# A graph convolution on one core: filters laid out by edge through TensorE alone, messages kept in SBUF, gathers released by the row sums

## What is computed

```python
def reference(x, src, dst, edge_attr_50, ...):
    h = jnp.maximum(_layernorm(x), 0.0)
    W = silu(edge_attr_50 @ fw1 + fb1) @ fw2 + fb2      # a filter for each edge, 50 -> 128 -> 128
    y = silu(h @ aw1 + ab1) @ aw2 + ab2                 # the node table
    msg = W * y[src]
    agg = jax.ops.segment_sum(msg, dst, num_segments=6250)
    out = silu(agg @ ow1 + ob1) @ ow2 + ob2
    return x + h + out
```

## Time and profile before

| what | value |
|---|---|
| time, median of 3 (lowest, highest) | 2037.55 us (2035.7, 2040.6) |
| span of the profiled execution, first to last instruction | 2356.9 us |
| POOL busy in it | 1526.1 us, 65% |
| PE busy in it | 1290.8 us, 55% |
| DVE busy in it | 1191.7 us, 51% |
| ACT busy in it | 520.7 us, 22% |
| TensorE clock granted, mean | 0.741 of full speed |

### The profile page before, as it was taken

The page is one execution under the profiler, slowest core; times in us unless marked ns, Lnnn a source line. Parts: engine busy times, 40 slices in busy tenths (PEclk is TensorE's granted clock), DMA queues, the critical chain, the costliest instruction groups (busy, mean ns, idle before and its releaser), DMA issues.

```text
span 2356.9 us, 13198 instructions
## 1 busy us (share of the span) xinstructions
PE 1290.8 (55%) x4526; PEld 700.7 (30%) x4526; DVE 1191.7 (51%) x1497; ACT 520.7 (22%) x545; POOL 1526.1 (65%) x1619
## 2 busy tenths in 40 slices
PE   3454555655565557555655565555564566554645
PEld 2222333332232323223322232222232233322323
DVE  4455445555455445544544564445444454444545
ACT  3322222222121122122212221222121122121211
POOL 5556666667666666666666666666666676666665
PEclk9686777777786768776877786777686777677867
DMA  4421222212221212212212221222221222212211
GB/s 148 144 76 45 82 58 71 79 51 85 82 83 45 83 50 81 87 46 81 86 51 78 80 85 50 80 65 65 82 85 48 82 54 81 85 45 82 59 46 44
DMA packets 62293, 171.47 MB, mean 73 GB/s; under 512 B 27088, under 2 KB 29648, under 8 KB 59024
## 3 DMA queue, kind: packets, MB, share of 16 engines
q0 software_dynamic: 51584, 105.75, 16.8%
q1 hardware_dynamic: 8192, 61.32, 6.9%
q10 hardware_dynamic: 2448, 3.54, 0.4%
HBM read 164.08 MB, written 6.42 MB: 72 GB/s over the span
## 4 chain that ended last, share of the span: by engine, by line
another core or an unknown queue 30%; POOL 24%; PE 18%; issue 16%; ACT 9%; DVE 2%; DMA 0%; SPq 0%; POOLq 0%; ACTq 0%; DVEq 0%
POOL xg L381 24%; PE banks L884 9%; PE banks L876 4%; ACT hid L444 4%; ACT hid L450 4%; PE banks L891 2%; PE banks L824 1%; PE banks L899 1%; ACT hs L469 0%; DVE stats L557 0%; PE banks L819 0%; DMA xs<-in_x 0%; PE banks L944 0%; DVE sums L668 0%
## 5 line engine op out<-in xcount | busy, mean ns | idle before, releaser
L381 POOL DMA_INDIRECT xg<-node_table,src x1564 | 1479.0, 946 | 777.6 <-issue 451.3
L884 PE MATMUL banks<-hid,wts 128*128 128x512 f32 x806 | 534.4, 798 | 556.3 <-ACT hid L444 437.9
L665 DVE TENSOR_TENSOR banks<-banks,xg 128x1024 f32<-128x1024 f32 (+1 forms) x198 | 241.4, 1219 | 1070.2 <-DMA xg<-node_table,src 607.2
L668 DVE TENSOR_REDUCE sums<-banks 128x128 f32<-128x1024 f32 (+1 forms) x408 | 494.0, 1211 | 13.7
L876 PE MATMUL banks<-attr,wts 50*128 50x512 f32 x806 | 284.4, 786 | 383.1 <-ACT hid L450 206.4
L444 ACT ACTIVATE hid<-banks,cols 128x1024 f32<-128x1024 f32 x202 | 224.7, 1112 | 887.9 <-remote 672.4
L450 ACT ACTIVATE hid<-banks,cols 128x1024 f32<-128x1024 f32 x202 | 224.6, 1112 | 865.6 <-remote 376.6
L884 PEld LDWEIGHTS banks<-hid,wts 128*128 128x128 f32 x806 | 180.6, 249 | 746.6 <-ACT hid L444 465.7
L891 PE MATMUL banks<-ident,hid 128*128 128x128 f32 x1612 | 283.5, 333 | 40.1 <-issue 38.1
L891 PEld LDWEIGHTS banks<-ident,hid 128*128 128x128 f32 x1612 | 224.6, 170 | 237.1 <-issue 228.6
L672 DVE TENSOR_TENSOR banks<-banks,other 128x1024 f32<-128x1024 f32 (+1 forms) x204 | 248.7, 1219 | 7.0
(11 more groups left out here) (83 smaller groups left out, 282.9 us busy)
## 6 DMA issues: line engine op xcount, KB each, us to landing
attr<-in_attr SPq DMA_DIRECT2D x25, 2048.0 KB
xg<-node_table,src POOLq DMA_INDIRECT x1564
out<-res ACTq DMA_DIRECT2D x8, 256.0 KB
xs<-in_x SPq DMA_DIRECT2D x3, 512.0 KB, 6.6
node_table<-res SPq DMA_DIRECT2D x3, 512.0 KB
out<-res ACTq DMA_DIRECT2D x5, 192.0 KB
spare<-in_dst SPq DMA_DIRECT2D x1, 808.0 KB
src<-in_src SPq DMA_DIRECT2D x1, 808.0 KB
```

What stands on the lines that cost most here:

```text
L381: pool.indirect_dma_start(xg[:, i % XG, j, :], None, table[:, :], bass.IndirectOffsetOnAxis(ap=src[:, s * L + j:s * L + j + 1], axis=0))\
L665: dve.tensor_tensor(to, to, rows_of, ALU.mult).then_inc(signal, 1)
L668: return dve.reduce_sum(sums[:, at, m, :], of.rearrange("p j f -> p f j"), AX.X)
L884: i = pe.matmul(hid_ps[:, at], w["fw2_s"][:, :], hid[:, s % 2, at], start=True, stop=True)
```

## The change

It does five things.

1. `filters` now makes the filters by edge directly. For each tile of 128 edges the hidden values are the stationary operand and `fw2` the moving one, 128 wide, eight matmuls into `fil_ps[s % 2]`. The bias comes first, as two bf16 matmuls 512 wide of a row block `fb2_rows` that holds `fb2` in three bf16 parts. `by_edge` (the transposes) and ScalarE's `add_fb2` go, and with them `across`, `biased` and `fil_done`.
2. The hidden layer runs `FILL` = 2 pairs ahead. One semaphore, `pe_turn`, is added to once a turn, by `hidden(s + 2)`, which stands behind `filters(s)`; all who waited for one of TensorE's semaphores in the loop wait for it, the node MLP's steps too (`turn_of`, `after`).
3. The message is written over the gathered rows in `xg` (in `e_x` for early pairs) in SBUF, and masked there; both row sums read it there.
4. `filters(s)` waits for `msg_done` of pair `s - 2`, and `pair_sums(a)` for `red_done` of its own pair. POOL waits for `red_done` of the pair that last used its buffer, three sets back, and no longer for the filters of the pair before.
5. `fb2_rows` is built on VectorE at the start, ahead of the node statistics (eight small instructions and a wait for the `rows` load); before, this stood in the fallback.

```diff
@@ POOL
                 if i >= XG:
-                    pool.wait_ge(fil_done, run(s - REACH))
+                    pool.wait_ge(red_done, run(MAIN_TURNS[i - XG]))
@@ ScalarE
-                for a in ((0, 1) if s == 0 else (s + 1,)):
+                for a in range(FILL + 1) if s == 0 else (s + FILL,):
                     if a < PAIRS:
                         silu_hid(a)
-                        add_fb2(a)
@@ VectorE, head
+            dve.wait_ge(s_rows, 16)
+            dve.wait_ge(s_set, 1)
+            dve.tensor_copy(fb2_part[:, 0, :], rows[:, 0, :]).then_inc(s_fb2, 1)
+            dve.wait_ge(s_fb2, 1)
+            dve.tensor_tensor(fb2_rest[:, 0, :], rows[:, 0, :], fb2_part[:, 0, :], ALU.subtract).then_inc(s_fb2, 1)
...
+            for i in range(3):
+                dve.tensor_copy(fb2_rows[32 * i:32 * i + 1, :, :],
+                                fb2_part[32 * i:32 * i + 1, i:i + 1, :].to_broadcast([1, TPG, F])).then_inc(s_fb2, 1)
@@ VectorE, loop
-            def message(to, rows_of, signal):
-                dve.tensor_tensor(to, to, rows_of, ALU.mult).then_inc(signal, 1)
+            def message(to, filters_of, signal):
+                dve.tensor_tensor(to, filters_of, to, ALU.mult).then_inc(signal, 1)
...
-                dve.wait_ge(fil_done, run(s))
-                msg = by_tile(s, 0, L)
-                message(msg, rows_of, msg_done)
+                dve.wait_ge(pe_turn, after(s))
+                msg = rows_of
+                message(msg, by_tile(s, 0, L), msg_done)
@@ TensorE
                 if s > 0:
-                    pe.wait_ge(biased, run(s - 1))
+                    pe.wait_ge(hid_done, run(s - 1))
...
-                i.then_inc(hid_sum, 1)
+                i.then_inc(pe_turn, 1)
             def filters(s):
+                to, halves = fil_ps[s % 2], range(tiles_in(s) // TPG)
+                pe.wait_ge(msg_done, run(s, LAG))
+                for h in halves:
+                    pe.matmul(to[:, GC * h:GC * h + GC], ones_b[:, :], fb2_rows.rearrange("p j f -> p (j f)"), start=True, stop=False)
                 pe.wait_ge(hid_done, run(s))
-                for h in range(tiles_in(s) // TPG):
-                    at = slice(GC * h, GC * h + GC)
-                    i = pe.matmul(hid_ps[:, at], w["fw2_s"][:, :], hid[:, s % 2, at], start=True, stop=True)
-                i.then_inc(across, 1)
-            def by_edge(s):
                 for j in range(tiles_in(s)):
                     at = slice(j * P, (j + 1) * P)
-                    i = pe.transpose(fil_ps[s % 2][:, at], hid[:, s % 2, at], ident[:, :])
-                i.then_inc(fil_done, 1)
+                    i = pe.matmul(to[:, at], hid[:, s % 2, at], w["fw2_s"][:, :], start=False, stop=j % TPG == TPG - 1)
+                return i
```

More of the change, by code:

```diff
@@ L150, in table_writes, with turn_of @@
     return sum(len(transfers(i)) for i in range(c + 1))
+def turn_of(kind, n, step):
+    return TASKS[TASK_OF[kind, n]][2] + (EARLY_STEPS if kind == "early" else OUT_STEPS)[step]
 def turns(pair, task):
@@ L173, in run, with after @@
     return c + (1 + AHEAD - d)
+def after(s):
+    return run(s + FILL)
 def gnn_layer(nc, x, e_src_t, src_t, dst_t, attr_t, node_wts_t, wts_t, cols_t, rows_t, out):
@@ L398, in _ @@
             act.dma_start(cols[:, :], cols_t).then_inc(s_cols, 16)
-            for ahead in (s_h, s_mid, a_mid, hid_done, biased):
+            for ahead in (s_h, s_mid, a_mid, hid_done):
                 act.sem_inc(ahead, AHEAD)
@@ L442, in silu_hid @@
                 n = tiles_in(s) * P
-                act.wait_ge(hid_sum, run(s))
+                act.wait_ge(pe_turn, run(s))
                 act.activation(hid[:, s % 2, 0:n], hid_ps[:, 0:n], ACT.Silu, bias=cols[:, 0:1]).then_inc(hid_done, 1)
-            def add_fb2(s):
-                n = tiles_in(s) * P
-                act.wait_ge(across, run(s))
-                act.activation(hid[:, s % 2, 0:n], hid_ps[:, 0:n], ACT.Identity, bias=cols[:, 3:4]).then_inc(biased, 1)
             def pair(s):
-                for a in ((0, 1) if s == 0 else (s + 1,)):
+                for a in range(FILL + 1) if s == 0 else (s + FILL,):
                     if a < PAIRS:
                         silu_hid(a)
-                        add_fb2(a)
                 if s == STD_TURN:
@@ L473, in task @@
                     width, bias = (GC, 1) if kind == "early" else (OUTS[n][1] * P, 2)
-                    act.wait_ge(n_l1, b + 1)
-                    if b > 0:
-                        act.wait_ge(n_l2, b)
-                    source = last_ps_1 if kind == "out" and n == len(OUTS) - 1 else node_ps
+                    last = kind == "out" and n == len(OUTS) - 1
+                    if last:
+                        act.wait_ge(last_l1, 1)
+                    else:
+                        act.wait_ge(pe_turn, after(turn_of(kind, n, "middle")))
+                    source = last_ps_1 if last else node_ps
                     act.activation(mid[:, 0:width], source[:, 0:width], ACT.Silu, bias=cols[:, bias:bias + 1])\
@@ L716, in by_halves @@
                 i, k, n = MAIN_OF[s], HALVED.index(s), tiles_in(s) // 2
-                dve.wait_ge(fil_done, run(s))
+                dve.wait_ge(pe_turn, after(s))
                 for h in range(2):
-                    msg, done = by_tile(s, h, n), 2 * k + h + 1
+                    msg, done = xg[:, i % XG, n * h:n * h + n, :], 2 * k + h + 1
                     dve.wait_ge(half_gathered[2 * k + h], 16 * n)
-                    message(msg, xg[:, i % XG, n * h:n * h + n, :], half_msg)
+                    message(msg, by_tile(s, h, n), half_msg)
                     dve.wait_ge(half_msg, done)
@@ L733, in task @@
                 if step == "copied":
-                    dve.wait_ge(n_tr, n + 1)
+                    dve.wait_ge(pe_turn, after(turn_of(kind, n, "copied")))
                     dve.tensor_copy(hT[:, 0:GC], node_ps).then_inc(n_hT, 1)
                 elif step == "rows" and kind == "early":
-                    dve.wait_ge(n_l2, b + 1)
+                    dve.wait_ge(pe_turn, after(turn_of(kind, n, "rows")))
                     dve.tensor_tensor(e_x[:, n * TPG:(n + 1) * TPG, :], node_ps.rearrange("p (j f) -> p j f", f=F),
@@ L747, in task @@
                     if to is yc:
-                        dve.wait_ge(n_l2, b + 1)
+                        dve.wait_ge(pe_turn, after(turn_of(kind, n, "rows")))
                     dve.tensor_tensor(to, to, rows[:, 2:3, :].to_broadcast([P, tiles, F]), ALU.add).then_inc(s_xs, 1)
                     if to is xc:
-                        dve.wait_ge(n_l2, b + 1)
+                        dve.wait_ge(last_l2, 1)
                     if n >= 2:
@@ L846, in node_layer2 @@
                 pe.wait_ge(s_res, run(c, 1))
-                layer2(l2_ps, TILES[c], w["aw2_s"][:, :], s_l2)
-            for ahead in (s_tr, s_l1, s_l2, a_l1, a_l2, hid_sum, across, fil_done):
+                layer2(l2_ps, TILES[c], w["aw2_s"][:, :]).then_inc(s_l2, 1)
+            for ahead in (s_tr, s_l1, s_l2, a_l1, a_l2, pe_turn):
                 pe.sem_inc(ahead, AHEAD)
@@ L860, in _ @@
             pe.wait_ge(s_set, 1)
+            pe.wait_ge(s_fb2, 8)
             pe.wait_ge(s_res, run(N_CHUNKS - 1))
@@ L914, in pair @@
                 if s == 0:
-                    hidden(s)
-                    filters(s)
-                if s + 1 < PAIRS:
-                    hidden(s + 1)
-                else:
-                    pe.wait_ge(biased, run(s))
-                pe.wait_ge(red_done, run(s, LAG))
-                by_edge(s)
-                if s + 1 < PAIRS:
-                    filters(s + 1)
+                    for a in range(FILL):
+                        hidden(a)
+                i = filters(s)
+                if s + FILL < PAIRS:
+                    hidden(s + FILL)
+                else:
+                    i.then_inc(pe_turn, 1)
                 for a in SUMS_AT.get(s, ()):
+                    pe.wait_ge(red_done, run(a))
                     pair_sums(a)
```

67 lines of the change are left out of this document (31 added, 36 removed).

## The result

| what | before | after |
|---|---|---|
| time, median (lowest, highest), 4 runs each | 2038.88 us (2035.7, 2040.6) | 2147.3 us (2144.07, 2151.84) |
| ratio, 95% interval | | 1.0533 [1.0517, 1.0549] |
| profiled execution: span, its own time | 2356.9 us, not known | 2150.0 us, 2151.84 us |

The change makes the kernel 5.3% slower, 108 us. The forecast was 2110 us with 2018 to 2190 around it. In the profiled execution of after the time and the span differ by 1.8 us, so this time the profile can be read as it stands.

What follows compares the result with a forecast made beforehand. POOL's back-to-back gathers, 10.0 us a turn, were taken as the bound. 2037.55 - 6 (POOL's new wait) + 76 (masks) + 2.4 (head) = 2110 us; range 2018 to 2190, the forecast's own 2060 to 2170.

Steps and rivals of the forecast that it cites:

- POOL is the bound, 1.25 us a gather: POOL's loop: one gather costs 0.946 + 0.305 us, eight 10.0 us, and a turn cannot be shorter.
- The 316.5 us of waits in the earlier trace: POOL's 90 waits in the profile before: executions without a profile hardly have them, leaving 0 to 18 us.
- POOL's new wait, -6 us: POOL waiting for row sums three sets back: gains what was still waited for, 0 to 18 us, taken as 6.
- TensorE and ScalarE, 0 us: TensorE net -0.6 us a turn, -120 us in all; ScalarE loses `add_fb2`, 224.6 us; both off the path.
- The head, +2.4 us: Start of kernel: eight small VectorE instructions ahead of the statistics delay the first gather 2.4 us, ends 0 and 4.
- The masks, +76 us: Loop masks with two SBUF inputs hold up POOL's gathers: 0.39 us on 195 sets, 76 us, ends 12 and 187.
- The rule for one collision: POOL's gather is late by the time from its start to the DVE instruction's end, less 0.13 us.
- The average over phases: Mask cost averaged over a gather period of 1.25 us, the mask's start not being fixed: 0.40 us.
- Rival A: Masks keep the harmless phase against gathers: 2046 us, or 2034 without stragglers; chance 0.27.
- Rival B: TensorE's late increments are in every run, POOL's issue shorter unprofiled: about 1905 us, half mixture 2015; chance 0.14.
- Rival C: Masks lock in the worst phase, 0.1 to 0.4 us before a gather: 187 us, 2221 us; chance 0.10.
- Rival D: VectorE becomes the bound if row sums from SBUF take over 2.8 times as long; with others, chance 0.04.

Runs made afterwards that it cites:

- the shifted mask: Changed kernel with an unused VectorE reduction of 453 columns between the first row sum and the mask; 2178.07 us, ratio 1.0696 on the 2037 chip.

## Why the forecast held, point by point

- **POOL is the bound, 1.25 us a gather: right.** 0.944 + 0.305 us in every kernel without collisions.
- **The 316.5 us of waits in the earlier trace rows are not in the median: right for these runs, in all likelihood wrong in its cause.** I put them down to the recording. But the four profiled kernels on the 2037 chip have none of them, the kernel before can have at most some 7 us of them there (what the new wait saved), and on the two others it takes 2334 us and more in every run. So the profile and the median of before came, as far as is known, from chips of different kinds. Taking 316.5 us off the span landed on the median because these waits are nearly all of the difference, and not because a recording adds them: that much of the forecast's hit is luck.
- **POOL's new wait, -6 us: right**, -6.6 us measured; no wait for another engine was left in the loop.
- **TensorE and ScalarE, 0 us: right**, -0.1 us with the head. ScalarE is busy 296.7 us (about 300 forecast). TensorE is busy 1209.2 us and not 1170: the filters' matmuls take 363 ns where line 824 had 323. The bias matmuls, two a turn, were put at 0.42 us each by a row 491 wide and show 549 ns. It all lies under POOL.
- **The head, +2.4 us: the step itself right, its path wrong.** The statistics start at 9.95 instead of 7.78 us, 2.2 us later. But on the 2037 chip the loop's first gather is at 64.08 us in the changed kernel and at 64.10 us in the one with only POOL's wait. POOL issues the 48 early gathers back to back from 3.8 us to 64 us, and that covers the table. Only just: in the result's own trace the first gather waits 1.2 us for it and starts at 65.27 us. I had looked at a profile in which late increments had pushed the first gather to 95.7 us.
- **The masks, +76 us: right in kind, its size too small.** The rule for one collision held from 0.04 to 1.1 us. The average over phases did not: 117.0 us in time, 114.5 and 118.1 us in the traces. The step that failed was "where in a gather's period the mask begins is not fixed": it is fixed to within 0.2 us in three turns of four (151 of 202). The trace of before could have told: 99 of its 116 messages that wait for a landing start 1.5 to 1.75 us behind the end of their set's last gather, as they do after the change. "If it is under way for less than about 0.1 us the gather was seen to win" holds for the short line 655 in the trace of before, and not for masks: those under way for 0.04 to 0.1 us cost 0.98 to 1.05 us each. The average itself was worked out as 0.40 us and entered as 0.39, and there are 196 sets, not 195; that is 2 us. I had allowed 5.5 to 8.0 us a turn for VectorE and judged that "the sum would be the same"; only POOL's bound is the same. The 0.68 us by which the first row sum is longer sets the mask's phase, and so the cost of most, at 0.59 us.
- **Rival A** (harmless phase) falls to that same 0.68 us. An estimate: the masks' places in the kernel with the message in PSUM, priced by the rule, come to about 26 us. **Rival B** had half of a truth: on two of three chips the late increments' cost is in every run. But there the three sets of room make the kernel slower, not faster, and its shorter issue, 1.05 us a gather without a profile, exists nowhere: a run's time and its span agree within 2 us. **Rival C** asked for masks 0.1 to 0.4 us ahead of a start; the shifted mask came near it, at 2178 us against the 2221 forecast. **Rival D:** row sums are 1.53 times as long, not 2.8.

The best kernels found on the 2037 chip are the one before with POOL's wait alone and the changed one with the message in PSUM, both 0.3% faster. Kernels with that wait are 10.7% and 9.5% slower on the 2341 and the 2354 chip, so neither is a version to put in place unless the chips are known.

## What to carry to other kernels

An operand moved from PSUM to SBUF has a price outside its own instruction. Where GpSimd issues gathers back to back and is the bound, a VectorE instruction with two SBUF inputs that is under way at a gather's start delays that gather and all that follow, and by how much depends on the exact durations ahead of it: from the gather's end to its landing, and of each instruction in between. Price such edits with the sum of those durations and not with an average over phases. Before the idle time of a profile is believed, or thrown away, compare its span with the time of that very execution. If the two agree and yet stand off the other times, the difference is not the recording's, and may belong to the chip on which the profile was taken.

## What of the hardware was not expected

- **A gather is held by a VectorE instruction with two SBUF inputs, up to 1.07 us each.** With one input in SBUF, whether the result goes to SBUF or to PSUM, 0.00 us at any distance. VectorE is not held in turn: in the result's trace 178 of 200 masks start while a gather runs, and none lasts over 1.26 us. The Trainium skill (SBUF — State Buffer, Who interferes with whom) says that such an instruction contends with a GpSimd instruction that reads SBUF, over a port pair that is an exclusive lock. The traces agree for the gather, above all with the mask that started 0.06 us ahead of one and held it for 1.03 us; that a gather holds a mask no run here shows. The remark of the Trainium skill in the same section that `tensor_tensor` was not seen to stall DMAs does not hold for these indirect ones: it cost 117 us.
- **A reduction over fp32 with a step of 512 bytes takes 1.88 us from SBUF and 1.22 us from PSUM**, for 1024 elements a partition. 453 elements in a row took 0.61 us from SBUF, 1.35 ns each with the start; with the step it was 1.84 ns each. The Trainium skill (SBUF — State Buffer, Door 1) says that each access that crosses to a new 16-byte line pays; the traces agree in direction.
- **Messages start in step with the gathers by a coincidence of durations.** On the 2037 chip 144 of 200 start within 0.2 us behind the start of a later gather in the changed kernel (125 in the result's trace, where 45 more start just ahead of one). They start some 1.6 us behind the end of the last gather they need, and with its own 0.94 us that is nearly two gather periods of 1.25 us.
- **One chip and two others differ by 15% on the same kernel**, 2036.73 against 2341.0 and 2353.64 us, in every run. TensorE's own work is not longer there: with POOL's wait alone changed it is busy 1293.1 us on the 2037 chip and 1293.9 us on the 2341 chip, at a mean granted clock of 0.790 and 0.719. On the slower ones ScalarE, VectorE and POOL often go on several microseconds after TensorE's last matmul record (for VectorE 967.52 against 974.45 us in the timeline above). Whether the increment is late or TensorE's own end, these traces cannot tell, since ends of matmuls are modelled. That stays open.
